# A three-layer pair-product network: the first layer's pairs packed into six full tiles and a stacked remainder, and one group of the second layer subtracted on GpSimd instead of VectorE

## The reference

```python
h = x                                             # (512, 39, 16)
for i, S in enumerate([128, 128, 128]):
    Wr = Ws[i].reshape(39, h.shape[1], S)
    out = relu(einsum('bfd,bgd,fgs->bsd', x, h, Wr) + bs[i][None, :, None])
    if i != 2: h, direct = out[:, :64], out[:, 64:]
    else:      direct = out
    outs.append(direct)
return sum(concatenate(outs, axis=1), axis=-1)    # (512, 256)
```

## Time and profile before

| | |
|---|---|
| runs | 589.92, 589.99, 590.31 us |
| the profiled execution | 589.6 us, its span 587.8 us |
| TensorE clock granted, mean | 0.985 |
| busy: TensorE, VectorE, GpSimd, ScalarE | 559.3, 535.4, 517.4, 375.5 us |
| HBM traffic | 207 GB/s over the span |

### The profile page before, as it was taken

One profiled execution on the slowest core, in us unless ns is written; L12 is line 12 of the kernel. 1 busy time (PEld: TensorE's weight loads), 2 busy tenths in 40 slices (PEclk: granted clock), 3 DMA queues, 4 the chain that ended last, 5 costly groups with the idle time before them and its releaser, 6 DMA issues.

```text
span 587.8 us, 7877 instructions
## 1 busy us (share of the span) xinstructions
PE 559.3 (95%) x2032; PEld 384.8 (65%) x2032; DVE 535.4 (91%) x514; ACT 375.5 (64%) x421; POOL 517.4 (88%) x231
## 2 busy tenths in 40 slices
PE   1795999999999999999999999999999999999997
PEld 0363666676767667676766767676676767667765
DVE  3665989999999999999999999999999999999975
ACT  2555567585766758576675857667585766758663
POOL 1593997989899898989989898998989899898995
PEclk9797999999999999999999999999999999999999
DMA  8997651845749285574818557392855738163001
GB/s 309 420 418 281 227 214 64 302 183 167 300 129 339 72 295 200 166 298 131 341 66 295 202 166 298 126 342 70 294 204 167 297 134 336 68 212 106 0 3 36
DMA packets 26787, 121.61 MB, mean 207 GB/s; under 512 B 3242, under 2 KB 3370, under 8 KB 24468
## 3 DMA queue, kind: packets, MB, share of 16 engines
q1 hardware_dynamic: 26772, 121.44, 57.1%
HBM read 120.90 MB, written 0.52 MB: 207 GB/s over the span
## 4 chain that ended last, share of the span: by engine, by line
PE 87%; POOL 5%; issue 4%; DMA 1%; DVE 1%; ACT 1%; SPq 0%; POOLq 0%; ACTq 0%
PE acc L451 87%; POOL z_lo L223 5%; DMA xfirst<-x 1%; DVE z_raw L334 0%; ACT h L521 0%; ACT last L521 0%; DVE z_whole L334 0%; ACT z_hi L518 0%; DVE z_hi L221 0%; DVE sums L357 0%; ACT xrep_psum L538 0%; DVE z_lo L220 0%; SPq L252 0%; SPq L253 0%; POOLq L212 0%
## 5 line engine op out<-in xcount | busy, mean ns | idle before, releaser
L223 POOL TENSOR_TENSOR z_lo<-z_raw,z_hi 128x1024 fp32r<-128x1024 f32 (+2 forms) x224 | 511.6, 2323 | 53.9 <-ACT z_hi L518 53.9
L518 ACT CAST z_hi<-z_raw 128x1024 fp32r<-128x1024 f32 (+2 forms) x224 | 224.9, 1017 | 115.6 <-DVE z_raw L334 84.2
L334 DVE TENSOR_TENSOR z_raw<-h,xwide 128x1024 f32<-128x1024 f32 x192 | 229.9, 1218 | 19.8 <-ACT h L521 16.4
L451 PE MATMUL acc<-z_hi,w_hi 128*128 128x512 f32 (+2 forms) x560 | 222.9, 467 | 7.8 <-ACT z_hi L518 7.1
L451 PE MATMUL acc<-z_hi,w_lo 128*128 128x512 f32 (+2 forms) x560 | 183.4, 397 | 0.0
L451 PE MATMUL acc<-z_lo,w_hi 128*128 128x512 f32 (+1 forms) x528 | 171.9, 399 | 5.6 <-DVE z_hi L221 3.3
L451 PEld LDWEIGHTS acc<-z_hi,w_hi 128*128 128x128 f32 (+2 forms) x560 | 106.2, 190 | 69.6 <-issue 50.1
L451 PEld LDWEIGHTS acc<-z_hi,w_lo 128*128 128x128 f32 (+2 forms) x560 | 105.9, 189 | 28.6 <-issue 3.8
L451 PE MATMUL acc<-z_whole,w_whole 128*128 128x512 f32 x256 | 122.3, 601 | 0.0
L451 PEld LDWEIGHTS acc<-z_lo,w_hi 128*128 128x128 f32 (+1 forms) x528 | 99.0, 189 | 33.0 <-POOL z_lo L223 5.3
L334 DVE TENSOR_TENSOR z_psum<-h,xwide 128x1024 f32<-128x1024 f32 x64 | 78.3, 1224 | 0.1
(11 more groups left out here) (16 smaller groups left out, 90.8 us busy)
## 6 DMA issues: line engine op xcount, KB each, us to landing
xwide<-x SPq DMA_DIRECT2D x160, 512.0 KB, 4.7
xfirst<-x SPq DMA_DIRECT2D x15, 2048.0 KB, 7.8
xwide<-w SPq DMA_DIRECT2D x2, 1024.0 KB, 13.4
xfirst<-x SPq DMA_DIRECT2D x1, 1280.0 KB, 8.1
xfirst<-x SPq DMA_DIRECT2D x1, 768.0 KB, 9.6
w_whole<-w_rest SPq DMA_DIRECT2D x1, 512.0 KB, 11.5
w<-w0a SPq DMA_DIRECT2D x1, 409.5 KB
direct<-w0b SPq DMA_DIRECT2D x1, 409.5 KB
```

What stands on the lines that cost most here:

```text
L223: return eng.tensor_tensor(lo[0:rows, 0:n, :], z[0:rows, 0:n, :], hi[0:rows, 0:n, :].bitcast(F32), ALU.subtract)
L334: nc.vector.tensor_tensor(dst, in0, in1, ALU.mult).then_inc(made[kind], 1)
L451: return nc.tensor.matmul(dst, w[0:rows, PLACE[layer, t], :], z[0:rows, t - G * g, :], start=first and t == 0, stop=final and t == TILES[l ...
L518: nc.scalar.copy(z_hi[0:rows, slot("PV", pair, par, pos, HI_RING), 0:n, :], src).then_inc(hi_made, 1)
```

## The change

Layer 0's 780 pairs fill six tiles of 128 rows, and the 12 pairs that are left stand three times in the seventh, at rows 0, 32 and 64 (76 rows with the gaps). Its group, 0.3 at place 16, becomes a V: ScalarE casts all the rows to z_hi, VectorE overwrites rows 32 to 43 with the low part, and the weights of rows 64 to 75 are the low part of the weights, made once at the start by VectorE. One matmul then does for this tile what three did. Group 1.6 (the seventh of the second layer, place 9) becomes a P: its product goes to z_raw, and GpSimd subtracts. The host lays x0 and the weights out by `pair_places`. Tiles 0 to 5 of layer 0 have 128 rows instead of 117 on all engines. SCHEDULE, the rings and the loads stay.

```diff
--- before.py
+++ after.py
@@ -20,11 +20,12 @@
 PAIRS = BLOCKS // 2
 BB = N // DIM
 
-SHIFTS = FIELDS // 2 + 1
-PER = 3
-T0 = -(-SHIFTS // PER)
-P0 = PER * FIELDS
-P0_LAST = (SHIFTS - PER * (T0 - 1)) * FIELDS
+PAIRS0 = FIELDS * (FIELDS + 1) // 2
+T0 = PAIRS0 // 128 + 1
+LEFT = PAIRS0 - 128 * (T0 - 1)
+P0_LAST = 64 + LEFT
 T12 = -(-FIELDS // 2)
 G = 2
 TILES = (T0, T12, T12)
@@ -35,7 +36,7 @@
 
 
 
-KINDS = ("WPWP", "PWPWPPVPPV", "PPWPVPPWPV") 
+KINDS = ("WPWV", "PWPWPPPPPV", "PPWPVPPWPV") 
 G12 = len(KINDS[1])
 SCHEDULE = "111112100122221001212222"
 
@@ -89,8 +90,48 @@
 
 def rows_of(layer, t):
     if layer == 0:
-        return P0 if t < T0 - 1 else P0_LAST
+        return 128 if t < T0 - 1 else P0_LAST
     return 128
+def row_fields():
+    fields = [None] * 128
+    for first in (0, 32, 64):
+        fields[first:first + LEFT] = range(LEFT)
+    rest = [f for f in range(LEFT, FIELDS) for _ in range(3)]
+    rest += range(LEFT, LEFT + fields.count(None) - len(rest))
+    for p in range(128):
+        if fields[p] is None:
+            fields[p] = rest.pop(0)
+    return fields
+def pair_places():
+    fields = row_fields()
+    room = [[(p, t) for t in range(T0 - 1) for p in range(128) if fields[p] == f] + [(f, T0 - 1)] * (f < LEFT)
+            for f in range(FIELDS)]
+    held = [[] for _ in range(FIELDS)]
+    def put(pair, tried):
+        for f in pair:
+            if f not in tried:
+                tried.add(f)
+                if len(held[f]) < len(room[f]):
+                    held[f].append(pair)
+                    return True
+                for other in list(held[f]):
+                    if put(other, tried):
+                        held[f].remove(other)
+                        held[f].append(pair)
+                        return True
+        return False
+    for a in range(FIELDS):
+        for b in range(a, FIELDS):
+            assert put((a, b), set())
+    return [(p, t, f, pair[0] + pair[1] - f) for f in range(FIELDS) for (p, t), pair in zip(room[f], held[f])]
 
 
 def weight_places():
@@ -133,14 +174,14 @@
         def sem(name):
             return ctx.enter_context(nc.semaphore(name))
 
-        w0 = sb("w0", [P0, T0, SIZE])
+        w0 = sb("w0", [128, T0, SIZE])
         w_whole = sb("w_whole", [128, N_WHOLE, SIZE])
         w_hi = sb("w_hi", [128, N_SPLIT, SIZE], F32R)
         w_lo = sb("w_lo", [128, N_SPLIT, SIZE], F32R)
         bias = sb("bias", [128, 3])
 
         xfirst = sb("xfirst", [128, 1 + T0, N])
-        xshift = xfirst[0:P0, 1:1 + T0, :]
+        xshift = xfirst[:, 1:1 + T0, :]
         xwide = sb("xwide", [128, 2, T12, N])
         z_whole = sb("z_whole", [128, WHOLE_RING, G, N])
         z_raw = sb("z_raw", [128, RAW_RING, G, N])
@@ -159,7 +200,7 @@
 
         stage = [None, xwide[:, 1, T12 - 4:T12, :].rearrange("p a (b s) -> p (a b) s", s=SIZE),
                  xwide[:, 1, T12 - 8:T12 - 4, :].rearrange("p a (b s) -> p (a b) s", s=SIZE)]
-        w0t = direct[:].rearrange("p a (b s) -> p (a b) s", s=SIZE)[0:P0, 0:T0, :]
+        w0t = direct[:].rearrange("p a (b s) -> p (a b) s", s=SIZE)[:, 0:T0, :]
 
         w0_in = sem("w0_in")
         w0_folded = sem("w0_folded")
@@ -167,6 +208,7 @@
         w_whole_in = sem("w_whole_in")
         w_hi_made = sem("w_hi_made")
         w_lo_made = sem("w_lo_made")
+        w0_third_made = sem("w0_third_made")
         w1_lo_made = sem("w1_lo_made")
         bias_in = sem("bias_in")
         xfirst_in = sem("xfirst_in")
@@ -214,7 +256,11 @@
         def take(eng, z, hi, lo, layer, g):
 
             n = len(tiles_of(layer, g))
-            rows = P0 if layer == 0 else 128
+            rows = rows_of(layer, G * g)
+            if layer == 0 and g == len(KINDS[0]) - 1:
+                second = slice(32, 32 + LEFT)
+                return eng.tensor_tensor(hi[second, 0, :], z[second, 0, :], hi[second, 0, :].bitcast(F32),
+                                         ALU.subtract)
             if layer and g == G12 - 1:
                 under = slice(HALF, 128)
                 eng.tensor_tensor(lo[:, 0:n - 1, :], z[:, 0:n - 1, :], hi[:, 0:n - 1, :].bitcast(F32), ALU.subtract)
@@ -270,7 +316,7 @@
             sp.wait_ge(*made_all(0, 0))
             load_first(2, xfirst_in)
             sp.wait_ge(w1_lo_made, 1)
-            sp.wait_ge(w_lo_made, len(SPLIT0) + 1)
+            sp.wait_ge(w_lo_made, len(SPLIT0))
             for g in range(ASIDE, G12):
                 load_wide(1, 1, g)
             for par in range(2):
@@ -305,8 +351,8 @@
                         dve.wait_ge(xfirst_head_in, 16)
                     elif g == (2 if first else 0):
                         dve.wait_ge(xfirst_in, 16 * (j + 2))
-                    in0 = xrep_psum[0:P0, None, :].to_broadcast([P0, n, N])
-                    in1 = xshift[:, G * g:G * g + n, :]
+                    in0 = xrep_psum[0:rows, None, :].to_broadcast([rows, n, N])
+                    in1 = xshift[0:rows, G * g:G * g + n, :]
                 elif layer == 1:
                     if g == 0:
                         dve.wait_ge(h_ready[0], 2 * (j + 1))
@@ -381,6 +427,12 @@
             nc.vector.tensor_tensor(w0[:], w0[:], w0t, ALU.add).then_inc(w0_folded, 1)
             for pos in range(len(order(-1))):
                 products(-1, 0, pos)
+            a, third = SPLIT0[-1][0], slice(64, 64 + LEFT)
+            dve.wait_ge(w_hi_made, len(SPLIT0))
+            nc.vector.tensor_tensor(w_hi[third, a, :], w0[third, T0 - 1, :], w_hi[third, a, :].bitcast(F32),
+                                    ALU.subtract).then_inc(w0_third_made, 1)
+            subtract(-1, 0, len(order(-1)) - 1)
             a, n = SPLIT_FROM[1], SPLIT_COUNT[1]
             dve.wait_ge(w_hi_made, len(SPLIT0) + 1)
             nc.vector.tensor_tensor(w_lo[:, a:a + n, :], stage[1][:, 0:n, :], w_hi[:, a:a + n, :].bitcast(F32),
@@ -423,8 +475,8 @@
                 nc.gpsimd.tensor_tensor(w_lo[0:rows, a:a + n, :], raw, w_hi[0:rows, a:a + n, :].bitcast(F32),
                                         ALU.subtract).then_inc(w_lo_made, 1)
 
-            for i, (a, ts) in enumerate(SPLIT0):
-                split(w0[:, ts[0]:ts[-1] + 1, :], a, len(ts), P0, i + 1)
+            for i, (a, ts) in enumerate(SPLIT0[:-1]):
+                split(w0[:, ts[0]:ts[-1] + 1, :], a, len(ts), 128, i + 1)
             for par in range(2):
                 step(-1, par)
             for par in range(2):
@@ -454,7 +506,7 @@
 
                 if g == 0:
                     if layer == 2 and isinstance(j, int) and j == 1:
-                        pe.wait_ge(w_lo_made, len(SPLIT0) + 1)
+                        pe.wait_ge(w_lo_made, len(SPLIT0))
 
                     ready(pe, acc_read[layer], j + (1, 0, -1)[layer])
                 if kind == "W":
@@ -465,9 +517,15 @@
                     mm.then_inc(whole_used, 1)
                     return
                 if isinstance(j, int) and j == -1:
-                    pe.wait_ge(w_lo_made, len(SPLIT0))
+                    pe.wait_ge(w_lo_made, len(SPLIT0) - 1)
+                    if last_g:
+                        pe.wait_ge(w0_third_made, 1)
                 pe.wait_ge(hi_made, before("PV", j, pos) + 1)
                 hi = z_hi[:, slot("PV", pair, par, pos, HI_RING)]
+                if layer == 0 and last_g:
+                    pe.wait_ge(lo_made[kind], number + 1)
+                    matmul(w_hi, hi, ts[0], True, True).then_inc(split_used, 1)
+                    return
                 stacked = ts[-1] if layer and last_g else None
                 ts = [t for t in ts if t != stacked]
                 for t in ts:
@@ -535,7 +593,7 @@
                     act.wait_ge(xfirst_in, 16 * (j + 2))
                 if not isinstance(j, int) or j >= 0:
                     act.wait_ge(*made_all(j - 1, 0))
-                nc.scalar.copy(xrep_psum[0:P0, :], xfirst[0:P0, 0, :]).then_inc(xrep_ready, 1)
+                nc.scalar.copy(xrep_psum[:], xfirst[:, 0, :]).then_inc(xrep_ready, 1)
 
             def relu0(j, half):
 
@@ -597,7 +655,7 @@
             copy_xrep(-1)
             act.wait_ge(w0_folded, 1)
             for a, ts in SPLIT0:
-                split(w0[:, ts[0]:ts[-1] + 1, :], a, len(ts), P0)
+                split(w0[:, ts[0]:ts[-1] + 1, :], a, len(ts), 128)
             for pos, (_, _, kind) in enumerate(order(-1)):
                 if kind != "W":
                     high_part(-1, 0, pos)
@@ -623,14 +681,17 @@
     x = np.asarray(r_x).transpose(1, 0, 2).reshape(FIELDS, BLOCKS, N).transpose(1, 0, 2)
     w0 = np.asarray(L0_rec_W0).reshape(FIELDS, FIELDS, SIZE)
 
-    w0a = np.zeros((PER, FIELDS, T0, SIZE), np.float32)
-    w0b = np.zeros((PER, FIELDS, T0, SIZE), np.float32)
-    f = np.arange(FIELDS)
-    for s in range(SHIFTS):
-        g = (f + s) % FIELDS
-        w0a[s // T0, :, s % T0] = w0[f, g]
-        if s:
-            w0b[s // T0, :, s % T0] = w0[g, f]
+    w0a = np.zeros((128, T0, SIZE), np.float32)
+    w0b = np.zeros((128, T0, SIZE), np.float32)
```

(17 more changed lines are left out.)

## The result

| | before | after |
|---|---|---|
| median of 5 runs | 589.99 us | 601.53 us |
| lowest to highest | 588.79 to 590.31 | 600.32 to 602.82 |
| profiled execution, span | 589.6, 587.8 | 600.32, 598.5 |

The ratio is 1.0205, with a 95% interval of 1.0186 to 1.0225: the change makes the kernel slower, 11.5 us by the medians. 601.2 was forecast.

A forecast was written before the change was run, and what follows sets the result against it. TensorE's own work (34.31 us a step) and a GpSimd-TensorE-ScalarE loop (34.21) nearly tie as bounds. Terms 7.5 + 1.3 + 2.4 = 11.2 us led to 601.2 us predicted; range 600 to 602.5, or 597 to 604 reaching into B and D.

The forecast's parts named there:

- Items 1 to 4: Full steps: fewer matmuls, moved subtractions and a later place 10 make a step 34.91 us for 34.30; plus 7.5 taken.
- the packing's gain: Layer 0's group 0.3: two matmuls less a block, 0.47 us a step, 7.5 us while TensorE is the bound.
- item 4: Place 10's subtraction becomes GpSimd's eighth, so place 11 starts 1.07 us later; a step grows to 34.91 us.
- The 0.5 us that the forecast took off its own 8.0: Full steps: plus 8.0 lowered to 7.5, as a free refill would give 6.7 and a 2.35 pace 7.5.
- item 3: Group 1.6's subtraction adds 2.36 us a step to GpSimd and takes 1.13 from VectorE, whose work falls by 0.4.
- Item 5: Before the loop: plus 1.4 in step 0, minus 0.35 in step 1, 0.3 for weight loads; plus 1.3 us.
- Item 6: After the loop, step 15: place 18 waits for GpSimd's eleventh subtraction instead of the tenth, plus 2.36 us.
- Item 7: Waits from the V at place 16, VectorE's raw-ring waits and later product 0 cost nothing.
- A: Rival: GpSimd's room is real and TensorE stays the bound, giving 582.5 us; chance 5%.
- B: Rival: pace or counted wait gives way, the loop is 0.3 to 0.6 us shorter, 593 to 597 us; chance 9%.
- C: Rival: each step's 1 us TensorE wait lowers the clock, losing 2.4 us a step, about 632 us; chance 3%.
- D: Rival: VectorE becomes the late one through place 16's V and raw-ring waits, adding 4 us, 605 us; chance 6%.

The follow-up runs named there:

- the change of order alone: The change with group 1.6 two places later in SCHEDULE, after 2.1 and 2.2, same instructions on every engine: 592.31 us, ratio to before 1.0041.
- the run with ScalarE's leg made shorter: The change with ScalarE's two activations into direct made after cast 0 instead of inside relu0 and relu1: 593.75 us, ratio to before 1.0069.
- the packing alone: The change with group 1.6 kept on VectorE and the stacked tile's 12-row subtraction made by GpSimd: 582.51 us, ratio to before 0.9877.
- the moved group alone: Kernel before with group 1.6 given to GpSimd, layer 0 unchanged, RAW_RING 5 and WHOLE_RING 3: 610.30 us, ratio 1.0341.
- the packing with ScalarE's leg made shorter: Group 1.6 kept on VectorE, GpSimd making the 12-row subtraction, plus ScalarE's two activations into direct after cast 0: 581.14 us, ratio to before 0.9850.

## Why the prediction was right

Against the profiled execution, by GpSimd's first starts of the steps:

| | forecast | measured |
|---|---|---|
| up to the start at 91.54 | +1.3 | 92.11 - 91.54 = +0.6 |
| 13 full steps | +7.5 (34.91 each less 0.5) | 453.6 - 445.8 = +7.8 (34.89 each) |
| from 537.34 to the end | +2.36 | 52.8 - 50.5 = +2.3 |
| sum, on a span of 587.8 | +11.2 | +10.7 |

*Items 1 to 4, the loop.* Confirmed at each joint: the place 11 start within 0.01 us, the wait at place 10 (0.83 where "some 0.9" stood), ScalarE's 7.3 us unchanged, and GpSimd idle 1.7 us a step, a little under the 1.9 named. The two experiments with one part each give both signs, and the change of order alone shows that place, not load, is what costs. The size of the packing's gain was right too, 7.5 against 7.0; it was only bought with a subtraction in front of place 10. That place had slack, but not enough: by the sum of item 4 the next group could start at 16.57 + 0.61 = 17.18 and did start at 18.46, so 1.28 us were there for a subtraction of 2.36. (The slack of 0.10 is that of place 6, which nothing was put in front of.) The 0.5 us that the forecast took off its own 8.0 was mostly not there: the wait's refill is real, the group after the waiting pair starts 0.58 after it (320.44 to 321.02) instead of 0.47.

Two small terms were wrong and carried nothing. Place 9 waits by the sum of item 4 for 17.18 - 17.07 = 0.11 us, not "about 0.3", and measured it is 0.12 (the next group starts at 318.67, due at 318.55). And VectorE's busy time in a step did not fall by the 0.4 of item 3: it is 33.22 us in both kernels.

*Item 5, the start,* was too high by 0.7. TensorE's rows tell where: relu0 of step 0 came 1.55 us later (47.26 for 45.71), as worked out with 1.4 plus the loads, yet step 1 began only 0.86 later (56.38 for 55.52). (From there to the next start it is 0.29 less, where minus 0.35 stood.) In between TensorE waits some 3 us for VectorE and then makes its last three matmuls of the step. In the kernel before it made them at the low clock:

```profile
50.78 0.80 PE L451 MATMUL acc<-z_lo,w_hi 128*128 128x512 f32 x1 [3.26 <-DVE z_hi L221]
...
51.81 0.63 PE L451 MATMUL acc<-z_hi,w_lo 128*128 128x512 f32 x1
```

and after the change at the high one, 0.97 us for 1.66 from the first start to the last end:

```profile
52.33 0.50 PE L503 MATMUL acc<-z_lo,w_hi 128*128 128x512 f32 x1 [3.25 <-DVE z_hi L267]
52.66 0.39 PE L503 MATMUL acc<-z_hi,w_hi 128*128 128x512 f32 x1
52.90 0.40 PE L503 MATMUL acc<-z_hi,w_lo 128*128 128x512 f32 x1
```

and the stretch's row (length, busy times, granted clock last but two) has 0.83, where the earlier trace rows has 0.51 for 50.0 to 55.6:

```profile
50.00:56.50 6.50, 1.02 (x4) 0.57 (x4) 4.07 (x5) 3.12 (x5) 0.12 (x1) 0.83 0.35 138
```

In after the clock fell as well, only later: it was 1.00 from 52 to 54, 0.58 from 54 to 56 and 0.50 from 56 to 60. This execution is the fastest of the five, by 1.2 us under the median, and has a mean clock of 0.989 where the others have 0.982. So the others ran longer at the low clock, but they have no trace, and where isn't shown. It can be at more than one place: in the trace of the run with ScalarE's leg made shorter, whose step 0 is the same program up to here, the clock fell during the waits for GpSimd, and the stretch from the pair that waited first to the last matmul before the wait for VectorE took 7.64 us (42.10 to 49.74) where it took 6.48 in after (42.21 to 48.69). That the median came out within 0.3 us of the forecast, nearer than the profiled execution, is luck: item 5 has no term for this.

*Item 6, the end:* the matmul at place 18 of step 15 waits for the eleventh subtraction.

```profile
571.80 0.72 PE L503 MATMUL acc<-z_lo,w_hi 128*128 128x512 f32 x2 [0.48 <-POOL z_lo L269]
```

It stands 26.06 after the start at 545.74, against 23.73 before.

*Item 7, what was costed at nothing,* held. VectorE's waits for the raw ring are there, and TensorE never waits for z_hi at place 16 (its waits for VectorE's z_hi are the same two as before, 4.3 us in all for the weight load):

```profile
310.98 1.22 DVE L380 TENSOR_TENSOR z_raw<-h,xwide 128x1024 f32<-128x1024 f32 x1 [0.63 <-POOL z_lo L269]
...
322.19 0.68 DVE L262 TENSOR_TENSOR z_hi<-z_psum,z_hi 12x512 fp32r<-12x512 f32 x1
```

The subtraction of 12 rows took 0.68 (0.70 taken, from 64 rows) and ends 5.4 us before its matmul at 328.24. The margin at relu1, which the forecast didn't look at, was thin: relu1 starts at 333.25, and place 19's last matmul, started at 332.61 and 0.40 long, ends at 333.01. It changes nothing here, and in the run with the shortened leg it is what stopped the gain.

*The rivals.* A is what the packing alone does, and needs group 1.6 to stay with VectorE. B is excluded by the 34.9 us steps. C: the waits of 0.8 us leave the granted clock at full; here a stretch that holds the wait at 320.44 (TensorE busy 33.63 of 34.30, clock 1.00):

```profile
297.27:331.57 34.30, 33.63 (x124) 22.88 (x123) 32.60 (x32) 22.48 (x27) 32.50 (x14) 1.00 0.58 207
```

The Trainium skill ("TensorE: Matmul & The Clock Gate", What's actually happening) has the throttled state as the default that activity releases. One wait of 0.8 us a step does not bring that state back here; around the 3 us waits at the start both traces show it, from about 50 us in the kernel before and from about 54 us in after. D did not come: VectorE is busy 33.22 us of a step of 34.90, and TensorE has no wait for it at place 16.

## What to carry to other kernels

Before work is moved to an engine with idle time, follow the dependences from one iteration to the next through all the engines, and count which operation of a burst each consumer waits for: an engine at 88% can leave 0.1 us of slack at one place and 1.3 at another, and a loop over three engines of which none is full can be longer than the busiest one's work. Costs of an order are mended by the order: the same instructions two places later gave back 9 of 11.5 us. Look at the branches that lie just under the longest path too: the one through place 19 had 0.24 us of margin, and took nearly half of the next gain. And cost the prologue and epilogue by their own orders and clock: apart from that branch, they held the errors.

## What was not expected of the hardware

TensorE's clock at one place of the program differs from trace to trace. The three matmuls after the wait of some 3 us in step 0 took 0.97 or 0.98 us in four traces (the change, the altered order, the moved group alone, and the packing with ScalarE's leg made shorter), 1.66 in that of before, and 1.16 to 1.42 in the other three. And where the first wait for GpSimd in step 0 was 1.90 us, the clock stayed at 1.00 (the change); where it was 2.14 and 2.16 (the change with ScalarE's leg made shorter, and the moved group alone), it had fallen by the next wait, which cost 1.2 and 2.8 us. With the altered order the wait there was 3.68 us and the clock stayed at 1.00, so the length of the wait alone does not decide it. And GpSimd's time for a subtraction doesn't depend on the rows in these traces: 12 x 512 took 1.30 us, 117 x 512 took 1.30 too.
